# A vision-transformer tower on one core: residual sums built on GpSimd, and the instruction lists reordered

## What is computed

```python
h = patches @ Wp.T + bp                                   # 16 x 36 x 192
h = layernorm(h + attention(h, w_qkv, w_out, b_out))      # 12 heads of 64, window of 65 keys, zero padding
h = layernorm(h + experts(h))                             # 3 causal single-head experts, 2 of 3 kept by a gate
# experts: (concat of weighted expert outputs) @ Wp + bp
```

## Time and profile before

| | |
|---|---|
| median of 3 runs | 114.96 us |
| profiled execution, own time | 115.59 us |
| its span | 113.8 us |
| TensorE matmul busy | 104.5 us (92%) |
| TensorE weight load busy | 93.7 us (82%) |
| VectorE busy | 76.7 us (67%) |
| ScalarE busy | 72.2 us (63%) |
| GpSimd busy | 21.5 us (19%) |

### The profile page before, as it was taken

One profiled execution on the slowest core, in us unless ns is written; L12 is line 12 of the kernel. 1 busy time (PEld: TensorE's weight loads), 2 busy tenths in 40 slices (PEclk: granted clock), 3 DMA queues, 4 the chain that ended last, 5 costly groups with the idle time before them and its releaser, 6 DMA issues.

```text
span 113.8 us, 3528 instructions
## 1 busy us (share of the span) xinstructions
PE 104.5 (92%) x1381; PEld 93.7 (82%) x1381; DVE 76.7 (67%) x240; ACT 72.2 (63%) x200; POOL 21.5 (19%) x34
## 2 busy tenths in 40 slices
PE   6999999999999999999999999999969878978940
PEld 4699899997799989799988998999958777876920
DVE  0565909276935787249585978887767779988661
ACT  4577784588898775946954378762366468539260
POOL 7003624554156500000493000000000000000000
PEclk9999999999999999999999999999999999999998
DMA  3999999200000000000000000000000000000202
GB/s 75 333 347 402 411 418 424 84 0 6 3 0 6 3 0 6 0 6 0 0 0 6 0 0 6 6 0 0 0 3 6 3 0 6 0 0 0 64 19 78
DMA packets 4124, 7.73 MB, mean 68 GB/s; under 512 B 1293, under 2 KB 2445, under 8 KB 3981
## 3 DMA queue, kind: packets, MB, share of 16 engines
q1 hardware_dynamic: 3740, 7.24, 17.6%
q10 hardware_dynamic: 368, 0.28, 0.7%
HBM read 7.08 MB, written 0.44 MB: 66 GB/s over the span
## 4 chain that ended last, share of the span: by engine, by line
PE 65%; DVE 16%; DMA 5%; issue 5%; ACT 3%; SPq 3%; DVEq 0%
PE proj L933 11%; PE score L1014 8%; PE outp L1059 7%; DMA x_f<-x_t 5%; PE outp L897 5%; PE proj L918 4%; PE trans L1038 4%; PE proj L925 3%; PE proj L919 3%; PE proj L922 3%; PE proj L926 3%; DVE wqk_f L759 2%; DVE ln_st L744 2%; ACT ln_ln L566 2%; SPq L375 1%
## 5 line engine op out<-in xcount | busy, mean ns | idle before, releaser
L545 ACT ACTIVATE pt_t<-trans,image_t 108x216 f32<-108x216 f32 (+1 forms) x42 | 14.6, 425 | 3.7 <-PE trans L1038 3.3
L1014 PE MATMUL score<-k_t,q_t 64*36 64x37 f32 (+1 forms) x416 | 10.5, 196 | 0.0
L1014 PEld LDWEIGHTS score<-k_t,q_t 64*36 64x36 f32 x416 | 9.0, 111 | 1.6 <-issue 1.0
L529 ACT ACTIVATE score<-d_t 128x296 f32<-128x296 f32 (+2 forms) x16 | 6.6, 413 | 5.8 <-DVE d_t L708 5.8
L705 DVE TENSOR_REDUCE mx_t<-score 128x8 f32<-128x296 f32 (+2 forms) x16 | 7.1, 444 | 4.5 <-PE score L1022 4.2
L718 DVE TENSOR_REDUCE sm_t<-score 128x8 f32<-128x288 f32 (+1 forms) x16 | 7.0, 438 | 4.2 <-ACT score L529 4.2
L566 ACT ACTIVATE ln_ln<-ln_mv,const 108x1 f32<-108x1 f32 (+1 forms) x12 | 3.6, 297 | 8.6 <-DVE ln_mv L747 8.6
L657 DVE TENSOR_TENSOR x_lo<-x_f,x_hi 128x288 fp32r<-128x288 f32 x12 | 6.3, 534 | 4.0 <-ACT x_hi L461 4.0
L505 ACT ACTIVATE q_t<-proj 128x288 f32<-128x288 f32 x12 | 5.0, 417 | 6.2 <-PE proj L926 5.9
L933 PE MATMUL proj<-wv_hi,h_hi 128*108 128x384 f32 (+1 forms) x24 | 8.2, 343 | 0.0
L418 POOL TENSOR_TENSOR wqk_lo<-wqk_f,wqk_hi 128x256 fp32r<-128x256 f32 x6 | 4.5, 756 | 18.1 <-ACT wqk_hi L465 18.1
(11 more groups left out here) (208 smaller groups left out, 341.5 us busy)
## 6 DMA issues: line engine op xcount, KB each, us to landing
ffn_f<-f_w SPq DMA_DIRECT2D x1, 1088.0 KB, 12.2
wqk_f<-w_qk SPq DMA_DIRECT2D x2, 512.0 KB, 8.2
x_f<-x_t SPq DMA_DIRECT2D x2, 432.0 KB, 6.5
wv_f<-w_v SPq DMA_DIRECT2D x1, 768.0 KB, 7.4
wo_f<-w_out SPq DMA_DIRECT2D x1, 768.0 KB, 9.9
x_f<-x_t SPq DMA_DIRECT2D x2, 288.0 KB, 4.8
tw_f<-tok_w SPq DMA_DIRECT2D x2, 256.0 KB, 4.6
wqk_f<-w_qk SPq DMA_DIRECT2D x2, 256.0 KB, 5.9
```

The costliest lines, as they stand in the source:

```text
L545: nc.scalar.activation(pt_t[:, n % 2, 0:tiles, :, i], trans[0:ROWS, 0:tiles, :, 0:TOK], ACT.Copy, scale=image_t[:, i:i + 1]).then_inc(spli ...
L1014: ins = nc.tensor.matmul(s[64 * h:64 * h + TOK, im, 0:width], q, k_t[rows, n % QK_RING, im, 0:width], start=(kind == "attn" and im == 0), ...
```

## The change

Seven edits in one diff:

1. GpSimd adds h hi, bias and h lo in fp32 into a new tile `h_res`, once for each group and layer (`residual_rows`), and `residual` puts this into the bank with two fp32 matmuls in transpose mode in place of five matmuls. `rows 0`, `br 0`, `diag`, `ones_f`, `ones_r`, `ident_r` and `rows_r` go.
2. The mask of `s n` is written by two matmuls of 64 rows each in place of one of 128.
3. `wo_*` have 192 columns a pair instead of 256, and the expert weights 1024 instead of 1088; the loads read 192-column slices.
4. The first x and `tw_f` come in five pieces instead of four; SyncE issues three `tw_f` pieces.
5. GpSimd's order: `pair_lo(3..5)` follow the others directly, then come the residual sums of both groups, the lo parts of the output weights and of the expert weights, and the residual sums of the second layer.
6. Two memsets of `ones_*` and two of their rows go.
7. The three lists are ordered anew.

```diff
-X_PIECES = [slice(0, 1), slice(1, 2), slice(2, 4), slice(4, 6)]
+X_PIECES = [slice(0, 1), slice(1, 2), slice(2, 3), slice(3, 4), slice(4, 6)]
-ACT_TOK, SP_TOK = (0, 1), (2, 3)
+ACT_TOK, SP_TOK = (0, 1), (2, 3, 4)
+RES_COLS = DIM - 128 + 2
...
 PE_ORDER, the first line before and after, and the last ones
-em 0, em 1, em 2, em 3, em 4, em 5, em 6, em 7, qk 0, em 8, qk 1, s 0, s 1, em 9, v 0 0, qk 2, em 10
+em 0, em 1, em 2, em 3, em 4, em 5, em 6, em 7, qk 0, em 8, qk 1, em 9, s 0, s 1, v 0 0, qk 2, em 10
...
-qk 15, t 13, fv 1 1, s 14, s 15, pv 13, res2 0 0, one2 0 0, t 14, res2 0 1, one2 0 1, out2 0 0, out2 0 1
-res2 0 2, one2 0 2, out2 0 2, t 15, pv 14, tr2 0, pv 15, res2 1 0, one2 1 0, res2 1 1, out2 1 0, one2 1 1
-out2 1 1, res2 1 2, one2 1 2, out2 1 2, tr2 1
+s 15, t 13, fv 1 1, pv 13, res2 0 0, res2 0 1, t 14, one2 0 0, res2 0 2, one2 0 1, out2 0 0, out2 0 1
+one2 0 2, out2 0 2, t 15, pv 14, tr2 0, pv 15, res2 1 0, one2 1 0, res2 1 1, one2 1 1, out2 1 0, out2 1 1
+res2 1 2, one2 1 2, out2 1 2, tr2 1
...
 ACT_ORDER, the first lines
-xs 0, xs 1, xs 2, xs 3, xs 4, xs 5, wq 0, xs 6, xs 7, wq 1, xs 8, hh 0, xs 9, cq 0, wv 0, cq 1, xs 10
-wq 2, cv 0 0, xs 11, cq 2, wq 3, ex 0, hh 1, cv 0 1, wq 4, ex 1, cv 0 2, sp 0, ex 2, cq 3, wq 5, sp 1
+xs 0, xs 1, xs 2, xs 3, xs 4, xs 5, wq 0, xs 6, xs 7, xs 8, wq 1, hh 0, xs 9, cq 0, wv 0, xs 10, wq 2
+cq 1, xs 11, wq 3, cv 0 0, wq 4, ex 0, wq 5, ex 1, cq 2, cv 0 1, hh 1, cv 0 2, cq 3, sp 0, ex 2, cq 4
...
 DVE_ORDER, from the gate of group 0
-sh 10, nm 9, nm 10, sh 11, cf 0 0, ol 7, ol 8, nm 11, cf 0 1, ol 9, ol 10, gd 0, ol 11, st 1 0, st 1 1
-ap 1 0, ap 1 1, st 1 2, ap 1 2, cn 12, h1 1, sh 12, nm 12, sh 13, gd 1, nm 13, cn 14, cf 1 0, ol 12
-cf 1 1, sh 14, sh 15, nm 14, ol 13, nm 15, st2 0 0, st2 0 1, st2 0 2, ap2 0 0, ap2 0 1, ap2 0 2, fin 0
-ol 14, ol 15, st2 1 0, st2 1 1, ap2 1 0, st2 1 2, ap2 1 1, ap2 1 2, fin 1
+sh 10, nm 9, nm 10, sh 11, ol 7, cf 0 0, ol 8, nm 11, ol 9, ol 10, gd 0, ol 11, cf 0 1, st 1 0, st 1 1
+ap 1 0, ap 1 1, st 1 2, ap 1 2, cn 12, h1 1, sh 12, sh 13, nm 12, gd 1, cn 14, nm 13, sh 14, cf 1 0, ol 12
+sh 15, nm 14, ol 13, cf 1 1, nm 15, st2 0 0, st2 0 1, st2 0 2, ap2 0 0, ap2 0 1, ap2 0 2, fin 0, ol 14
+ol 15, st2 1 0, st2 1 1, st2 1 2, ap2 1 0, ap2 1 1, ap2 1 2, fin 1
...
+            def residual_rows(g, lo_done, col):
+                pool.wait_ge(lo_done, NCH * g + NCH)
+                n = pool_sums[0]
+                pool_sums[0] += 1
+                for c in range(NCH):
+                    nc.gpsimd.tensor_tensor(h_res[:, g, c], hcols(h_hi, g, c).bitcast(F32),
+                                            bias[:, col + c:col + c + 1].broadcast_to([128, GT]), ALU.add).then_inc(biased, 1)
+                for c in range(NCH):
+                    pool.wait_ge(biased, NCH * n + c + 1)
+                    nc.gpsimd.tensor_tensor(h_res[:, g, c], h_res[:, g, c], hcols(h_lo, g, c).bitcast(F32),
+                                            ALU.add).then_inc(h_res_s, 1)
...
             for p in range(3, PAIRS):
                 pair_lo(p)
+            pool.wait_ge(ld_bias, 16)
+            for g in range(GROUPS):
+                residual_rows(g, h_lo_s, B_OUT)
             pool.wait_ge(wo_hi_s, 1)
...
             lo_part(ffn_lo[:], ffn_hi[:], ffn_f[:], ffn_lo_s, 0)
+            for g in range(GROUPS):
+                residual_rows(g, h1_lo_s, B_FFN)
...
                 if kind != "attn":
-                    nc.tensor.matmul(s[:, :, 0:width], idn, mask.unsqueeze(1).broadcast_to([128, slots, width]), start=True,
-                                     stop=False, skip_group_check=True)
+                    for h in range(2):
+                        rows = slice(HD * h, HD * h + HD)
+                        src = slice(0, HD) if halved(n) else rows
+                        nc.tensor.matmul(s[rows, :, 0:width], idn[src, src],
+                                         mask[src].unsqueeze(1).broadcast_to([HD, slots, width]), start=True, stop=False,
+                                         skip_group_check=True)
...
             def residual(b, g, t, layer):
-                rows = tile_rows(t)
-                pe.wait_ge(rows_s, 1)
-                nc.tensor.matmul(b[0:rows, 0:DIM], ones_r[:, 0:rows], rows_r[:, layer], start=True, stop=False,
-                                 skip_group_check=True)
-                for c, width in enumerate((128, 64)):
-                    for part in (h_hi, h_lo):
-                        nc.tensor.matmul(b[0:rows, 128 * c:128 * c + width], htile(part, c, g, t), ident_r[:, 0:width],
-                                         start=False, stop=False, skip_group_check=True)
+                rows, cols = tile_rows(t), tile_cols(t)
+                pe.wait_ge(h_res_s, NCH * (GROUPS * layer + g) + NCH)
+                for c, width in enumerate((128, RES_COLS)):
+                    nc.tensor.matmul(b[0:rows, 128 * c:128 * c + width], h_res[0:width, g, c, cols],
+                                     ident[0:width, 0:width], start=(c == 0), stop=False, is_transpose=True,
+                                     skip_group_check=True)
```

More of the change, by code:

```diff
@@ L111 @@
-outb 1 1, outa 1 2, outb 1 2, qk 12, tr 1, qk 13, s 12, gate 1, s 13, lg 1, t 12, qk 14, fv 1 0, pv 12
-qk 15, t 13, fv 1 1, s 14, s 15, pv 13, res2 0 0, one2 0 0, t 14, res2 0 1, one2 0 1, out2 0 0, out2 0 1
-res2 0 2, one2 0 2, out2 0 2, t 15, pv 14, tr2 0, pv 15, res2 1 0, one2 1 0, res2 1 1, out2 1 0, one2 1 1
-out2 1 1, res2 1 2, one2 1 2, out2 1 2, tr2 1
+em 0, em 1, em 2, em 3, em 4, em 5, em 6, em 7, qk 0, em 8, qk 1, em 9, s 0, s 1, v 0 0, qk 2, em 10
+v 0 1, em 11, v 0 2, qk 3, t 0, s 2, s 3, t 1, qk 4, v 1 0, pv 0, pv 1, s 4, t 2, qk 5, t 3, qk 6, s 5
@@ new lines @@
+pv 2, pv 3, s 6, t 4, v 1 1, v 1 2, t 5, qk 7, pv 4, pv 5, s 7, qk 8, outa 0 0, t 6, outb 0 0, outa 0 1
+outb 0 1, outa 0 2, t 7, outb 0 2, qk 9, s 8, tr 0, pv 6, pv 7, qk 10, s 9, s 10, t 8, gate 0, qk 11, pv 8
+t 9, s 11, fv 0 0, t 10, lg 0, pv 9, pv 10, fv 0 1, t 11, outa 1 0, pv 11, outa 1 1, outb 1 0, outb 1 1
+outa 1 2, outb 1 2, qk 12, tr 1, qk 13, s 12, gate 1, s 13, lg 1, qk 14, qk 15, t 12, fv 1 0, s 14, pv 12
+s 15, t 13, fv 1 1, pv 13, res2 0 0, res2 0 1, t 14, one2 0 0, res2 0 2, one2 0 1, out2 0 0, out2 0 1
@@ L165, in vit_tower @@
         wv_lo = sb("wv_lo", [128, PATCH], F32R)
-        wo_f = sb("wo_f", [128, PAIRS, DUP])
-        wo_hi = sb("wo_hi", [128, PAIRS, DUP], F32R)
-        wo_lo = sb("wo_lo", [128, PAIRS, DUP], F32R)
+        wo_f = sb("wo_f", [128, PAIRS, DIM])
+        wo_hi = sb("wo_hi", [128, PAIRS, DIM], F32R)
+        wo_lo = sb("wo_lo", [128, PAIRS, DIM], F32R)
         ffn_f = sb("ffn_f", [128, NCH, F_END])
@@ L253, in vit_tower @@
         h_hi_s, h_lo_s = sem("h_hi_s"), sem("h_lo_s")
-        diag_s, ident_s, rows_hi_s, rows_s = (sem(s) for s in ("diag_s", "ident_s", "rows_hi_s", "rows_s"))
+        h_res_s, biased = sem("h_res_s"), sem("biased")
         projected, summed = sem("projected"), sem("summed")
@@ L314, in vit_tower @@
                         ready[(kind, (key, z))] = n_projected
-            elif kind == "rows":
-                plan(kind, key, (rows_s, 1))
             elif kind == "gate":
@@ L365, in piece_of @@
             return [n for n, ks in enumerate((X_PIECES, X_LATER)[g]) if ks.start <= k < ks.stop][0]
-        ZEROED = 9
+        ZEROED = 5
         block = ctx.enter_context(nc.Block())
@@ L619, in _ @@
                     outputs_hi(*a)
-                elif kind == "br":
-                    bias_rows(*a)
                 elif kind in ("rs", "rs2"):
@@ L846, in _ @@
                     position_mask()
-                elif kind == "br":
-                    bias_rows_lo(*a)
                 elif kind == "sh":
@@ L1061, in outputs @@
                 ins.then_inc(attended, 1)
-            def bias_rows(n):
-                b = take("rows", n)
-                pe.wait_ge(diag_s, 4)
-                nc.tensor.matmul(b[:, 0:2 * DIM], ones_f[:], diag[:].rearrange("p l d -> p (l d)"), start=True,
-                                 stop=True).then_inc(projected, 1)
-            def residual(b, g, t, layer):
-                rows = tile_rows(t)
-                pe.wait_ge(rows_s, 1)
-                nc.tensor.matmul(b[0:rows, 0:DIM], ones_r[:, 0:rows], rows_r[:, layer], start=True, stop=False,
-                                 skip_group_check=True)
-                for c, width in enumerate((128, 64)):
-                    for part in (h_hi, h_lo):
-                        nc.tensor.matmul(b[0:rows, 128 * c:128 * c + width], htile(part, c, g, t), ident_r[:, 0:width],
-                                         start=False, stop=False, skip_group_check=True)
+            def residual(b, g, t, layer):
+                rows, cols = tile_rows(t), tile_cols(t)
[4 more added lines that the diff above has]
+                                     skip_group_check=True)
             def add_pair(b, g, t, p):
```

50 lines of the change are left out of this document (14 added, 36 removed).

## The result

The changed kernel takes 114.81 us (median of 20 executions, 113.75 to 120.09) against 115.31 of before: a ratio of 0.993, interval 0.9911 to 0.9949. That is 0.5 us faster where I had forecast 2.7, and outside the range. Ratios here leave out executions whose mean granted clock fell to 0.92 to 0.97, which the changed kernel and some of the experiments show more often than before does.

A forecast was written before the change was run, and what follows sets the result against it. TensorE was taken to bound 11.6 to 82.6 us, chains of waits with VectorE the end. 2.06 there + 0.82 tail - 0.2 head = 2.7 us off 115.59, so 112.9; against the median 112.3 us, range 111.3 to 113.1.

The forecast's parts named there:

- the head: First loads: two more issues delay later loads about 0.9 us, mostly hidden; 0.2 us lost, bounds 0 to 0.9.
- The residual's price: TensorE's residual as two fp32 transposes: 0.15 us for 108 tokens instead of 0.41, gaining 0.26.
- group 0 gives: Three residuals at `outa 0 t` in TensorE's dense stretch: 0.26 + 0.26 + 0.22 = 0.74 us gained.
- group 1 gave: Residuals at `outa 1 t`, partly behind a VectorE wait: 0.48 us gained together with the new list.
- The sign that I had named: Sign that the forecast is right: the step after `outb 0 2` starts some 1.6 us earlier.
- The tail's sum: After 82.6 us: 0.15 at `st2 0 0`, 0.24 at `out2 1 0`, 0.43 at `st2 1 2`, together 0.82 us gained.
- The 0.15 of `st2 0 0`: Tail: `st2 0 0` no longer waits for `out2 0 0`, as two residuals move into TensorE's idle time; 0.15 us gained.
- their end stays: VectorE's steps between the gate and `nm 15`: same steps reordered, without gaps, so no change in their end.
- 1: Rival, chance 0.20: the tail gives nothing, the dense stretch gives all; 1.9 us faster, 113.1 us.
- 2: Rival, chance 0.13: new lists give it back through `s 1`, a later load and serial masks, up to 2.4; 114.5 us.
- 4: Rival, chance 0.05: more than forecast, with transposes at 0.07, no head loss and lists closing small gaps; 110.8 us.
- 3: Rival, chance 0.07: GpSimd's sums hold VectorE up, including gate operations; some 5 us late, 117.2 us.

The follow-up runs named there:

- x1: The changed kernel with x and the embedding weights of group 0 in four pieces again: 114.02 us, ratio 0.987.
- x2: The kernel before with five pieces and nothing else changed: 116.37 us, ratio 1.0092.
- y5: The kernel before, four pieces, with two 16-byte loads issued ahead of the bias load, so all of group 1 loads later: 115.65 us, ratio 1.0008.
- x3: The kernel before with the new residual alone, without the bias-row steps; old lists, masks, weights and four pieces: 115.47 us, ratio 0.9998.
- x4: The changed kernel with four pieces and the old lists: 115.88 us over all executions, 115.33 without four at a low clock, ratio 1.0.
- y3: The changed kernel with four pieces and four more unread GpSimd sums behind each group's: 114.5 us in two executions, ratio 0.9918.
- z1: The kernel before with the changed kernel's three lists alone, bias row's step kept: 116.47 us in one execution at an undisturbed clock.

## Why the prediction was wrong

**The step that failed first: the head**, "a later issue is mostly hidden ... I take 0.2 lost". It cost 0.8 to 0.9 (x1, x2), the upper end of my bounds. I had argued with the queue for group 1's load. A queue hid half of that delay in the changed kernel (issued 1.01 us later, landed at 11.10 instead of 10.61), and a delay of 0.56 us costs nothing that shows (y5). I had not asked about the other thing moved: the last piece of group 0 is issued 0.95 to 1.01 us later too and is due at `em 4`, which waits for it (0.55 us in x2, 0.12 in the changed kernel) in these two kernels alone. And I took the smaller packets as a small change, where the rate over the first 12 us fell by 7 to 8% against before. The shares of these in the 0.8 to 0.9 stay open.

**The residual's price was right, its worth not.** 0.13 us between starts against the 0.15 predicted. Against before, `rows 0` and the lists give 1.02 in the changed kernel (`v 0 2` to `qk 5`; predicted 0.84) and group 0 gives 0.80 (`outa 0 0` to `qk 9`; 0.74). But 0.44 was given back between `qk 5` and `pv 4`, 0.10 up to `outa 1 0`, and group 1 gave 0.37 up to `lg 1` (0.48). The sign that I had named, the step after `outb 0 2` some 1.6 us earlier, came out at 0.40 (`qk 9`), or 1.13 with four pieces. I had read TensorE at 70.6 of 71.0 us as room for any saving "if the others keep up", and did not look at how far ahead they were. They were not ahead: x3 takes the same matmuls away and gains 0.31 us between `qk 0` and `lg 1`, x1 with the new lists 1.48. The gain needs both parts: shorter work, and lists that put other work where TensorE would now wait.

**The tail's sum was right to 0.01 us by luck, and something ahead of it was missed.** From `pv 15` to the last copy the offset goes from -0.35 to -1.16: 0.81. But this is 0.26 at `out2 1 0` and 0.55 at `st2 1 2`, priced at 0.24 + 0.43. The 0.15 of `st2 0 0` is not in it: its wait is gone, but it lies ahead of `pv 15`, and between `lg 1` and `pv 15` 0.32 was lost, against "their end stays". Of that, `oh 14` ahead of `rs2 0 2` is 0.17; the rest is open.

**Outside the span** 0.33 us were lost that no view shows. I had taken what lies around the span as a constant.

The account of the two profiled executions: forecast 2.68. Less by 0.78 in the head (0.98 at `v 0 2` for 0.20), 0.44 + 0.10 given back behind `qk 5`, 0.11 in group 1, 0.32 ahead of `pv 15`, 0.16 between the last copy and the end of the span (2.88 us before, 3.04 now), 0.41 outside the span; more by 0.18 at `qk 5` and 0.06 at `qk 9`. That leaves 0.60, and 115.59 - 115.0 is 0.59.

**The rivals.** 1 (the tail gives nothing) is refuted: it gave 0.81. 2 had a part of the mechanism: the five pieces cost 0.8 to 0.9, and the lists give 0.17 back at `oh 14`. Its two other places are wrong: `s 1` did not wait for `q_t`, and the masks cost nothing that shows (x3 and x4). 4 is refuted: the residual is at 0.13 and the head lost. 3 is refuted for this kernel and its mechanism is real (y3): its margin was the 0.98 us between GpSimd's end and the gate. It also shows on three small operations at 29.5 us, moved by the new list beside GpSimd's sums:

```profile
29.52 0.62 DVE L680 SCALAR_TENSOR_TENSOR posmask<-posb,const 128x36 f32<-128x36 f32 x1
30.06 0.66 DVE L684 TENSOR_TENSOR conv_b<-bias 64x1 f32<-64x1 f32 x1
30.75 0.72 DVE L687 TENSOR_TENSOR conv_b<-conv_b,bias 64x1 f32<-64x1 f32 x1
```

The last one adds 64 numbers in 0.72 us; in z1, without the sums, in 0.15. By the Trainium skill (SBUF — State Buffer, SBUF: two separate sides) a VectorE operation with two SBUF inputs and a GpSimd operation that reads SBUF exclude each other for a whole instruction; these rows and y3's agree, and the PSUM reader L804 that kept its time fits too.

## What to carry to other kernels

A busy engine at 99% tells that work is there, not how late the others may come: before pricing a cut at its full length, take for each following step the distance between when its last input is ready and when it starts, and count the cut only up to that. A load split in two issues the pieces behind it later and moves its own bytes in smaller packets; ask which of the pieces is due first. And price a change of lists and a change of work together, or test them apart in all four combinations: here, up to the gate, the two were worth 0.31 us and less than nothing, and together 1.48.
